# One 512-column bias addition and one reduction in place of four fused add-and-maximum instructions for each group of heads

## The reference

```python
q = (xn @ Wq).reshape(b, n, H, DH).transpose(0, 2, 1, 3)       # layer 1: l2-normalised, times q_scale
sim = jnp.einsum('bhid,bjd->bhij', q, k)                       # 128 x 129, with the null key's column
sim = sim + bias                                               # one 128 x 128 table for each head
sim = jnp.where(causal_mask, neg, sim)
sim = jnp.where(mask_p[:, None, None, :], sim, neg)
attn = jax.nn.softmax(sim, axis=-1)
out = jnp.einsum('bhij,bjd->bhid', attn, v)
return layernorm(out.transpose(0, 2, 1, 3).reshape(b, n, INNER) @ Wo, g_out)
```

## Time and profile before

| what | value |
|---|---|
| median of the runs | 1496.37 us |
| the profiled execution: span from first to last instruction | 1494.8 us |
| PE busy | 1388.4 us, 93% |
| DVE busy | 1258.5 us, 84% |
| ACT busy | 896.7 us, 60% |
| POOL busy | 816.0 us, 55% |
| mean granted clock of TensorE | 0.988 of full speed |

### The profile page before, as it was taken

The page is one execution under the profiler, slowest core; times in us unless marked ns, Lnnn a source line. Parts: engine busy times, 40 slices in busy tenths (PEclk is TensorE's granted clock), DMA queues, the critical chain, the costliest instruction groups (busy, mean ns, idle before and its releaser), DMA issues. The chain is left out here.

```text
span 1494.8 us, 31541 instructions
## 1 busy us (share of the span) xinstructions
PE 1388.4 (93%) x8792; PEld 1269.4 (85%) x8792; DVE 1258.5 (84%) x4794; ACT 896.7 (60%) x3125; POOL 816.0 (55%) x800
## 2 busy tenths in 40 slices
PE   1489999999999999999898999999999999999997
PEld 0388999999999999998787888888888888888886
DVE  4878877787778777878899999999999999899885
ACT  2265666666666666666665665665665665665663
POOL 2545444444444444444465666666665766766663
PEclk9799999999999999999999999999999999999999
DMA  5572011101110111011010110111010011011001
GB/s 162 180 135 72 28 35 42 42 29 35 42 42 29 35 42 42 29 34 43 22 43 26 40 42 29 34 42 35 28 42 35 28 42 37 26 42 42 21 30 36
DMA packets 43110, 68.01 MB, mean 46 GB/s; under 512 B 6080, under 2 KB 14272, under 8 KB 43072
## 3 DMA queue, kind: packets, MB, share of 16 engines
q1 hardware_dynamic: 41264, 65.18, 14.5%
q10 hardware_dynamic: 1808, 2.39, 0.6%
HBM read 48.68 MB, written 18.87 MB: 45 GB/s over the span
## 5 line engine op out<-in xcount | busy, mean ns | idle before, releaser
L439 POOL TENSOR_TENSOR bias_g<-bias,mask_row 128x512 f32<-128x512 f32 x256 | 330.2, 1290 | 375.4 <-DVE mx L900 222.5
L587 ACT ACTIVATE p_raw<-s_sb,neg_m 128x129 f32<-128x129 f32 x1024 | 398.5, 393 | 207.0 <-DVE neg_m L905 206.9
L447 POOL TENSOR_TENSOR p_sb<-p_raw,rden 128x512 f32<-128x512 f32 x256 | 267.3, 1044 | 177.7 <-DVE rden L911 177.7
L1040 PE MATMUL bank_q<-wq_h,xt_h 128*128 128x384 f32 (+1 forms) x768 | 264.8, 345 | 21.3 <-DVE xt_l L805 15.1
L1040 PE MATMUL bank_q<-wq_l,xt_h 128*128 128x384 f32 (+1 forms) x768 | 262.6, 342 | 0.0
L1040 PE MATMUL bank_q<-wq_h,xt_l 128*128 128x384 f32 (+1 forms) x768 | 261.3, 340 | 0.0
L900 DVE CUSTOM_DVE_ANT_0 s_sb<-bank_s,bias_g 128x128 f32<-128x128 f32 x1024 | 234.2, 282 | 0.2 <-issue 0.2
L1160 PE MATMUL bank_y<-wo_h,ot_h 128*128 128x512 f32 x512 | 219.1, 428 | 0.2 <-DVE ot_l L921 0.2
L1160 PE MATMUL bank_y<-wo_h,ot_l 128*128 128x512 f32 x512 | 202.8, 396 | 0.0
L1160 PE MATMUL bank_y<-wo_l,ot_h 128*128 128x512 f32 x512 | 201.1, 393 | 0.0
L915 DVE TENSOR_TENSOR pt_l<-bank_p,pt_h 128x512 fp32r<-128x512 f32 x256 | 174.7, 682 | 30.6 <-ACT pt_h L594 30.3
(11 more groups left out here) (112 smaller groups left out, 3148.8 us busy)
## 6 DMA issues: line engine op xcount, KB each, us to landing
x_in<-in_x SPq DMA_DIRECT2D x32, 256.0 KB, 2.6
x_res<-in_x SPq DMA_DIRECT2D x32, 256.0 KB, 2.6
x_mid<-y_out SPq DMA_DIRECT2D x32, 256.0 KB, 2.0
x_in<-x_mid SPq DMA_DIRECT2D x32, 256.0 KB, 2.6
x_res<-x_mid SPq DMA_DIRECT2D x32, 256.0 KB, 2.7
out_x<-y_out SPq DMA_DIRECT2D x32, 256.0 KB, 2.0
wq_raw<-in_L_cond_Wq SPq DMA_DIRECT2D x4, 768.0 KB, 6.3
wo_raw<-in_L_cond_Wo SPq DMA_DIRECT2D x1, 2048.0 KB, 9.0
```

Of the source, the lines that this page charges most:

```text
L439: e.tensor_tensor(bias_g[:, g % 2, :, :], bias[:, m[0], HG * g:HG * (g + 1), :], mask_row[:, :].unsqueeze(1).broadcast_to([P, HG, P]), ALU ...
L447: e.tensor_tensor(p_sb[:, g % 2, :, :], p_raw[:, g % 2, :, 0:P], r, ALU.mult).then_inc(p_ready[g], 1)
L587: last = e.activation(p_raw[:, g % 2, j, :], s_sb[:, g % 2, j, :], ACT.Exp, bias=neg_m[:, h:h + 1], accum_out=esum[:, h:h + 1])
L1040: last = e.matmul(out, a, b, start=(k == 0), stop=(k == len(passes) - 1))
```

## The change

In `scores` on DVE, the four fused instructions of a group (`tensor_tensor_reduce`, which adds the bias to 128 columns of scores and keeps the row's maximum in an accumulator that a second small instruction then reads out) become one `tensor_tensor` over all 512 columns of the group and one `reduce_max` over the same 512 columns, read back from SBUF. The semaphore `s_ready[g]` is now raised by the addition, before the maximum is taken. Two waits stand in the group instead of one: the reduction waits for `s_ready[g]`, and `neg_m` for a new semaphore, `mx_ready[g]`. The lines of the changed kernel are 20 lower than those of the kernel before, since blank lines at its head are gone.

```diff
+        mx_ready = sems("mx_ready", G)
...
                 e.tensor_scalar(s_sb[:, g % 2, :, P], nns[:, hs], -1.0, None, ALU.mult)
-                for j in range(HG):
-                    h = HG * g + j
-                    last = e.tensor_tensor_reduce(s_sb[:, g % 2, j, 0:P], bank_s[g % 2][:, j * P:(j + 1) * P],
-                                                  bias_g[:, g % 2, j, :], 1.0, LOWEST, ALU.add, ALU.max,
-                                                  mx[:, h:h + 1])
-                last.then_inc(s_ready[g], 1)
+                e.tensor_tensor(s_sb[:, g % 2, :, 0:P], bank_s[g % 2][:, :].rearrange("p (h j) -> p h j", h=HG),
+                                bias_g[:, g % 2, :, :], ALU.add).then_inc(s_ready[g], 1)
                 wait(e, s_ready[g], m)
+                e.reduce_max(mx[:, hs], s_sb[:, g % 2, :, 0:P], AX.X).then_inc(mx_ready[g], 1)
+                wait(e, mx_ready[g], m)
                 e.scalar_tensor_tensor(out=neg_m[:, hs], in0=mx[:, hs], scalar=-1.0, in1=nns[:, hs],
                                        op0=ALU.mult, op1=ALU.min).then_inc(neg_m_ready[g], 1)
```

More of the change, by code:

```diff
@@ L51 @@
 BIG = 1e38
-LOWEST = -3.4e38
 FIRST, LAST = 3, B - 4
```

## The result

The changed kernel takes 1536.93 us (1536.84 to 1537.75, four runs) against 1495.7 us for the kernel before (1495.02 to 1497.18, four runs), a ratio of 1.0273 with a 95% interval of 1.026 to 1.0286. It is 41 us slower. The forecast was 1511 us, with 0.27 for a case that came to 1540.6; it is that case that happened.

The account below looks back on a forecast made before the run. PE was taken to bound layer 0, a DVE, POOL, PE chain layer 1. 0.43 us in 32 steps (13.8) plus 1 us at the ends, 14.8 on the 1494.8 span, gave 1509.6, median 1511 us; range 1502 to 1543.

Parts of the forecast that it names:

- Bounds: Whole kernel: PE bounds layer 0, DVE having 62.7 us in 300 spare; a DVE, POOL, PE chain bounds layer 1.
- Cost of a group: Each group on DVE: addition, reduction and two waits take 1.43 us up to `neg_m`, 0.46 to 0.48 more.
- Group 0: Layer 1: POOL's mask job at 0.76, `neg_m` held to 2.07, the extra 0.47 hidden, group 1 starting 0.07 us earlier.
- `rden` 0.41 later: Layer 1, group 1: its uncovered extra 0.48 less 0.07 delays `rden` and POOL's run by 0.41 us (0.23 to 0.44).
- Group 3: Layer 1: `neg_m` due at 1008.75, POOL's product at 1008.76; 0.02 us a step lost if `neg_m` leads.
- `neg_m` first: Group 3, layer 1: `neg_m` starts before POOL's product, `q_nat` follows by 0.08; 1511 us (1503 to 1519), chance 0.50.
- POOL first: Rival, group 3, layer 1: POOL's product holds `neg_m`, 0.92 us a step more, together 1540.6 us; chance 0.27.
- Layer 0 pays nothing: Layer 0: PE's 0.51 us margin covers the 0.41 shift, cost zero; the rival of layer 0 paying had 1526, chance 0.10.
- Fewer instructions save time: Skill's rule for DVE: eight instructions turned into two should save time; the prediction said the fused timings don't bear it out.

Follow-up runs that it names:

- the kernels without the collision: The changed kernel with group 3 alone fused again, 1513.22 us, or with group 3's reduction negating over 129 columns and no `neg_m` operation, 1513.14 us.

## Why the prediction was wrong

Its terms, one by one:

- Bounds. Layer 0 PE, with spare time on DVE; layer 1 a chain through DVE, POOL and PE's transposes. Right: PE busy in layer 0 is unchanged, and all but some 2 us of the loss lies in layer 1's steps.
- Cost of a group: 1.43 us forecast; 1013.77 to 1015.21 is 1.44, and 1016.30 to 1017.74 is 1.44. Right to 0.01, and this 0.01 matters in group 3.
- Group 0: POOL at 0.76 (measured 0.76), `neg_m` held until 2.07 (2.08), group 1 at 2.51 (2.53). Right, within 0.02.
- `rden` 0.41 later: 4.05 for 3.61, 0.44. Right; the kernels without the collision show 0.44 a step for the forecast 0.43. For them alone 1511 would have been 2 us low.
- Group 3: "the two meet within 0.01 us, and either can be first. If `neg_m` is first, `q_nat` follows it by 0.08". The meeting came out to within 0.02. **This is the step that failed:** I gave `neg_m` first 0.50 and POOL first 0.27, took the former for the forecast, and so entered 0.02 us a step for group 3. POOL had it in 32 of 32 steps, `q_nat` started 0.98 after `neg_m` and not 0.08, and the term was 0.91 at `q_nat` (10.89 us after group 0, against 9.98 with group 3 fused) and 0.77 in the length of the step. The sum gave `neg_m` a lead of 0.01; with 1.44 for the group in place of 1.43 the lead is nothing, and measured it is 0.00, or 0.01 behind. My reason against POOL, the `neg_m` with its usual 0.16, spoke of a lead of 0.04. The sum was not fine enough to say which case it would be.
- All runs together show no grey zone at such a meeting with one of POOL's 512-column jobs. Every `neg_m` that started 0.02 us or more ahead was not held by the job (a lead of 0.02 once, 0.03 seven times, both with group 0 alone negated; 0.04 and 0.05 in over 200 cases); every one that started level or behind ended 0.01 to 0.03 after the job's end.
- The size of that case: 1540.6 forecast, 1536.9 measured. `q_nat` starts 0.98 after `neg_m` (1023.68 to 1024.66), and from group 0's addition to it 10.89 us go by instead of 9.55, 1.34 more, which is 0.41 + 0.92. But the step is only 1.21 longer. The collision costs 0.77 a step net (23.44 - 22.67). What gives 0.13 to 0.15 back lies behind it: PE's transposes of the two halves are 4.39 us apart (1025.31 to 1029.70) instead of 4.50. While PE waits, the work on DVE that it needs next catches up: POOL's product is over by then, so the two `v_l` take 0.34 us and not 0.72, and what stands behind them on DVE is 0.53 later than with group 3 fused, not 0.91. I had passed the loss on without that. It is read from the starts, not tested.
- Layer 0 pays nothing: right for this change in its loop (21.43 us a step before and after), though `neg_m` of group 2 lasted 0.98 us there in nearly every step, and the null column of group 3 1.04. With group 1 alone changed, 0.07 a step is seen there. The 23.4 us for a step, taken from the whole span, was too long for this layer; nothing hangs on it.
- "Fewer instructions save time", the rule weighed from the Trainium skill (VectorE: DVE Perf Modes, "Rules for kernel authors"): not here. The kernel with four 512-column additions and reductions and nothing else is 2.8 us slower than the fused one.

The rule of the exclusive lock (the Trainium skill, SBUF — State Buffer, "SBUF: two separate sides") fits `neg_m` against POOL's 512-column jobs in all of these runs: an operation with two SBUF inputs is held, and the negated reduction, with one, is not. It says that whichever starts first has the ports; at equal recorded starts POOL had them. Two measurements do not fit it. In the kernel before, `xn` started 0.03 us ahead of the mask job twice (76.02 for 76.05 and 773.67 for 773.70) and was held all the same, for 1.60 us in all; and POOL's power operation did not hold `neg_m` (last section).

## What to carry to other kernels

A tiny operation can last as long as a 512-column job of another engine, if the two share a port (here 1.05 us for 0.16); list which operations of the one can be held by the other, and compute where their starts fall. Where the sum puts two of them within a few hundredths of a microsecond, don't choose the cheap case: look for a version in which it doesn't matter, here a reduction that takes the null column in and negates. An addition that releases a waiting engine before the maximum is taken can pay for more work than it adds; it did so in group 0, in the fastest kernel of all, where the other three groups stay fused.

## What was not expected of the hardware

- POOL's power operation over six columns lasts 1.35 us, but `neg_m` in the middle of it (1020.56, with `rnorm` running from 1019.47 to 1020.82) takes 0.16. In the changed kernel 32 `neg_m` lie inside such an operation, and each takes 0.16 or 0.17. Only the jobs over 512 columns held it.
- The reduction over 516 columns took 0.69 us, as long as that over 512, so taking the null columns in was free.
- An engine that gets an extra operation of 0.10 us and a wait made the kernel 16 us faster, by moving one start 0.15 us.
